# Splitting the weighing of eight experts over VectorE, ScalarE and GpSimd

## The reference, cut to what matters

```
x = inputs.reshape(-1, d)                       # the normalised residual
gate = softmax(x @ gate_w + gate_b)
weights = gate * (gate >= 0.1)                  # then divided by their sum
out = 0
for e in range(8):
    out = out + weights[:, e:e + 1] * (x @ expert_w[e] + expert_b[e])
```

## Time and profile before

| what | value |
|---|---|
| median of three runs | 2033.2 us |
| the profiled execution | 2030.23 us |
| its span | 2028.4 us |
| VectorE busy | 1732.6 us, 85% |
| ScalarE busy | 1598.6 us, 79% |
| GpSimd busy | 1500.3 us, 74% |
| the expert block | 1594.5 to 1755.8 us of the span, 161.3 us |

### The profile page before, as it was taken

One profiled execution on the slowest core, in us unless ns is written; L12 is line 12 of the kernel. 1 busy time (PEld: TensorE's weight loads), 2 busy tenths in 40 slices (PEclk: granted clock), 3 DMA queues, 4 the chain that ended last, 5 costly groups with the idle time before them and its releaser, 6 DMA issues. The chain is left out here.

```text
span 2028.4 us, 26725 instructions
## 1 busy us (share of the span) xinstructions
PE 1588.8 (78%) x8579; PEld 560.5 (28%) x8579; DVE 1732.6 (85%) x3742; ACT 1598.6 (79%) x1374; POOL 1500.3 (74%) x1026
## 2 busy tenths in 40 slices
PE   2678888887788888768888888888887587899966
PEld 1122222222222222222222222222221243366655
DVE  3789999997999999879999999999997388755556
ACT  2689999998999999979999999999999311222243
POOL 2989999997999999889999999999998001000000
PEclk7789999998999999989999999999999787877778
DMA  4100000000000000010000000000000000000001
GB/s 112 29 28 13 13 13 18 13 13 27 29 13 13 13 17 15 12 39 14 18 13 12 13 18 13 13 13 19 13 13 7 1 1 0 0 1 1 1 0 42
DMA packets 32491, 33.12 MB, mean 16 GB/s; under 512 B 5657, under 2 KB 23136, under 8 KB 32352
## 3 DMA queue, kind: packets, MB, share of 16 engines
q1 hardware_dynamic: 31056, 31.06, 5.0%
q10 hardware_dynamic: 1296, 0.35, 0.1%
HBM read 22.74 MB, written 8.39 MB: 15 GB/s over the span
## 5 line engine op out<-in xcount | busy, mean ns | idle before, releaser
L879 POOL TENSOR_TENSOR sigma_weights<-grown 128x1024 f32<-128x1024 f32 x480 | 909.7, 1899 | 0.0
L792 ACT ACTIVATE tau_weights<-ps_tau 128x1024 f32<-128x1024 f32 x512 | 720.8, 1408 | 37.4 <-PE ps_tau L424 37.3
L573 DVE TENSOR_SCALAR sigma_weights<-ps_sig 128x512 int32<-128x512 int32 x1024 | 690.6, 674 | 62.8 <-PE ps_sig L415 62.3
L778 ACT ACTIVATE sigma_weights<-sigma_weights,kernel_shape 128x2048 f32<-128x2048 f32 x256 | 611.1, 2387 | 0.2 <-POOL sigma_weights L879 0.2
L582 DVE TENSOR_TENSOR running_max<-ps_sig,running_max 128x512 f32<-128x512 f32 x896 | 604.3, 674 | 0.0
L852 POOL TENSOR_SCALAR grown<-sigma_weights,kernel_shape 128x1024 f32<-128x1024 f32 x480 | 540.1, 1125 | 78.9 <-DVE sigma_weights L573 78.4
L787 ACT ACTIVATE sigma_weights<-sigma_weights 128x2048 f32<-128x2048 f32 x256 | 588.9, 2301 | 0.0
L466 PE MATMUL ps_acc<-sigma_weights,v_heads 128*9 128x512 f32 x2048 | 533.0, 599 | 0.0
L466 PE MATMUL ps_acc<-tau_weights,v_heads 128*9 128x512 f32 x2048 | 531.5, 598 | 0.6 <-DVE sums L599 0.5
L424 PE MATMUL ps_tau<-q_operand,k_operand 128*128 128x512 bf16 x1024 | 311.2, 386 | 207.7 <-ACT tau_weights L792 200.2
L415 PE MATMUL ps_sig<-q_operand,k_operand 96*128 96x512 bf16 x1024 | 402.0, 393 | 73.1 <-DVE running_max L582 43.8
(11 more groups left out here) (169 smaller groups left out, 1440.5 us busy)
## 6 DMA issues: line engine op xcount, KB each, us to landing
q_operand<-q_parts SPq DMA_DIRECT2D x192, 48.0 KB
k_operand<-k_parts SPq DMA_DIRECT2D x64, 144.0 KB
q_parts<-parts SPq DMA_DIRECT2D x24, 128.0 KB, 2.3
k_parts<-parts SPq DMA_DIRECT2D x24, 128.0 KB, 2.3
x_res<-in_L_attn_x SPq DMA_DIRECT2D x8, 256.0 KB, 5.4
q_operand<-max_rows SPq DMA_DIRECT2D x128, 2.0 KB
out<-x_res SPq DMA_DIRECT2D x4, 512.0 KB, 3.2
experts<-in_L_ffn_expert_w SPq DMA_DIRECT2D x1, 512.0 KB
```

What stands on the lines that cost most here:

```text
L573: dve.tensor_scalar(sig[:, g % SIG_RING, cols].bitcast(I32), ps_sig[:, half, :].bitcast(I32), SIGN_OFF, None, ALU.bitwise_and).then_inc(ma ...
L778: act.activation(chunk(c), chunk(c), ACT.Ln, bias=shape[:, CHUNK * c // TB % H, 1:2]).then_inc(ln_done, 1)
L792: act.activation(tau[:, g % TAU_RING, :], ps_tau[:, :, :].rearrange("p h q -> p (h q)"), ACT.Exp, scale=float(DH) ** -0.5).then_inc(tau_do ...
L879: pool.tensor_tensor(sig[:, g % SIG_RING, :], t, t, ALU.mult).then_inc(sq_ready, 1)
```

## The change

For each pair of tiles VectorE now weighs experts 0, 1, 2, 4, 5 and 6 (`OWN = 6`). The last expert of each half (3 and 7) is read out of PSUM by ScalarE, scaled by its weight and written to a new buffer `expert_scaled` in SBUF (four operations of 128x128 for a pair). GpSimd adds the two halves to each other and then adds the sum to x (two operations of 128x256 for a pair), after VectorE's own twelve of that pair and after both bias additions. `expert_scaled` has room for one pair, so ScalarE waits for GpSimd's addition of the pair before. ScalarE reads a bank only after VectorE's last read from it, and TensorE writes a bank again only when ScalarE has also read it.

ScalarE's list is cut in pieces: the scalings stand in it at the places of the pairs, and the copies for `biases`, `project` and `gate` stand between them. GpSimd's list gets eight new operations per batch around its old two.

```diff
--- before.py
+++ after.py
@@ -946,6 +946,7 @@
         guard = sb("gate_guard", [P, TB])
         weight = sb("gate_weight", [P, TB, E])
         weight_t = sb("gate_weight_t", [E, N])
+        scaled = sb("expert_scaled", [P, 2, 2, D])
         ps_t = ctx.enter_context(nc.psum_tensor("ps_mt", [P, 2, HALF], F32))
         ps_y = ctx.enter_context(nc.psum_tensor("ps_my", [P, 2, HALF], F32))
         ps_e = ctx.enter_context(nc.psum_tensor("ps_me", [P, 2, 2, HALF], F32))
@@ -958,6 +959,9 @@
         gate_ready, gate_step, exp_ready = sem("gate_ready"), sem("gate_step"), sem("gate_exp")
         bias_ready, bias_added = sem("expert_bias_ready"), sem("expert_bias_added")
         e_ready, e_step = sem("e_ready"), sem("e_step")
+        scaled_ready, scaled_summed, scaled_added = sem("e_scaled_ready"), sem("e_scaled_summed"), sem("e_scaled_added")
+
+        OWN = 6
         GATE = 11
         block = ctx.enter_context(nc.Block())
 
@@ -981,16 +985,33 @@
                     act.activation(turned_sb[:, use, g * HALF:(g + 1) * HALF], ps_t[:, g, :], ACT.Copy)\
                        .then_inc(turned_read, 1)
 
-            def normal_and_gate(b):
+            def scale(pair):
+                def part(b):
+                    act.wait_ge(gate_step, b * GATE + GATE)
+                    wait(act, scaled_added, b * 4 + pair)
+                    for half in range(2):
+                        for t in (2 * pair, 2 * pair + 1):
+                            act.wait_ge(e_step, b * TB * OWN + (2 * OWN * pair + OWN * half + OWN - 1 + t % 2))
+                            e = 4 * half + 3
+                            act.activation(scaled[:, t % 2, half, :], ps_e[:, t % 2, half, 3 * D:4 * D], ACT.Copy,
+                                           scale=weight[:, t, e:e + 1]).then_inc(scaled_ready, 1)
+                return part
+
+            def first_norm(b):
                 take_turned(b, 0, y_ready, b * TB)
                 take_rstd(act, w, mv[:, 0], lnv[:, 0], rstd[:, 0], mv_ready[0], ln_ready[0], rstd_ready[0], b)
+
+            def second_norm(b):
                 take_rstd(act, w, mv[:, 1], lnv[:, 1], rstd[:, 1], mv_ready[1], ln_ready[1], rstd_ready[1], b)
+
+            def gate(b):
                 take_turned(b, 1, e_ready, b * 2 * TB)
                 act.wait_ge(gate_step, b * GATE + 3)
                 act.activation(prob[:, :, :], lg[:, :, :], ACT.Exp).then_inc(exp_ready, 1)
 
             act.preload_act_table_set("natural_log_exp_and_others")
-            rounds(act, [(0, take_weights), (1, normal_and_gate)])
+            rounds(act, [(0, scale(0)), (0, take_weights), (0, scale(1)), (1, first_norm), (0, scale(2)), (1, second_norm),
+                         (0, scale(3)), (1, gate)])
 
         @block.tensor
         def _(pe):
@@ -1027,7 +1048,8 @@
 
                     for half in range(2):
 
-                        wait(pe, e_step, b * TB * E + max(0, 2 * E * (pair - 1) + E * (half + 1)))
+                        wait(pe, e_step, b * TB * OWN + max(0, 2 * OWN * (pair - 1) + OWN * (half + 1)))
+                        wait(pe, scaled_ready, b * 2 * TB + max(0, 4 * (pair - 1) + 2 * (half + 1)))
                         for t in (2 * pair, 2 * pair + 1):
                             pe.matmul(ps_e[:, t % 2, half, :], turned_sb[:, 1, t * P:(t + 1) * P],
                                       w["experts"][:, 4 * half:4 * half + 4, :], start=True, stop=True).then_inc(e_ready, 1)
@@ -1054,8 +1076,7 @@
 
                 return rows[:, :].unsqueeze(1).to_broadcast([P, TB, D])
 
-            for b in range(B):
-
+            def normed(b):
                 xs = w["x"][:, bass.ds(b * TB, TB), :]
                 pool.wait_ge(yn_ready, b * TB + TB)
                 pool.wait_ge(x_ready, b)
@@ -1064,6 +1085,22 @@
                 pool.wait_ge(x_step, b + 1)
                 alone(pool, w["pool_passed"])
                 pool.tensor_tensor(xs, xs, yn[:, :, :], ALU.add).then_inc(x_ready, 1)
+
+            def add_scaled(pair):
+                def part(b):
+                    pool.wait_ge(scaled_ready, b * 2 * TB + 4 * pair + 4)
+                    alone(pool, w["pool_passed"])
+                    pool.tensor_tensor(scaled[:, :, 0, :], scaled[:, :, 0, :], scaled[:, :, 1, :], ALU.add)\
+                        .then_inc(scaled_summed, 1)
+                    pool.wait_ge(scaled_summed, b * 4 + pair + 1)
+                    pool.wait_ge(bias_added, b * 2 + 2)
+                    pool.wait_ge(e_step, b * TB * OWN + 2 * OWN * (pair + 1))
+                    alone(pool, w["pool_passed"])
+                    two = w["x"][:, b * TB + 2 * pair:b * TB + 2 * pair + 2, :]
+                    pool.tensor_tensor(two, two, scaled[:, :, 0, :], ALU.add).then_inc(scaled_added, 1)
+                return part
+
+            rounds(pool, [(0, add_scaled(0)), (0, add_scaled(1)), (1, normed), (0, add_scaled(2)), (0, add_scaled(3))])
 
         @block.vector
         def _(dve):
@@ -1130,13 +1167,13 @@
             def experts(pair):
                 def part(b):
 
-                    done = 2 * E * pair
+                    done = 2 * OWN * pair
                     if pair == 1:
                         dve.wait_ge(bias_added, b * 2 + 2)
-                    for e in range(E):
+                    for e in (0, 1, 2, 4, 5, 6):
                         for t in (2 * pair, 2 * pair + 1):
                             if e > 0:
-                                dve.wait_ge(e_step, b * TB * E + (done - 1))
+                                dve.wait_ge(e_step, b * TB * OWN + (done - 1))
                             if e % 4 == 0:
                                 dve.wait_ge(e_ready, b * 2 * TB + (4 * pair + 2 * (e // 4) + t % 2 + 1))
                             dve.scalar_tensor_tensor(out=xt(b, t), in0=ps_e[:, t % 2, e // 4, (e % 4) * D:(e % 4 + 1) * D],
@@ -1147,7 +1184,7 @@
 
             def biases(b):
 
-                dve.wait_ge(e_step, b * TB * E + 2 * E)
+                dve.wait_ge(e_step, b * TB * OWN + 2 * OWN)
                 for g in range(2):
                     dve.wait_ge(bias_ready, b * TB + 4 * (g + 1))
                     xs = w["x"][:, bass.ds(b * TB + 4 * g, 4), :]
```

## The result

The changed kernel takes 2044.84 us (median of 4 runs, 2044.43 to 2048.99), the one before 2031.58 in the same comparison. The ratio is 1.0071 with a 95% interval of 1.0051 to 1.0091: slower, by 13 us (the medians) to 14 us (the ratio). The profiled execution took 2045.11 us with a span of 2043.3, 14.9 us above the 2028.4 of before.

The account below looks back on a forecast made before the run. VectorE's list bounds the expert block, with ScalarE's copies hidden beside it. Three rounds of 43.60 us add 18.7 us and the last batch 1.9: +20.6, forecast 2051 us, own range 2045 to 2057, whole range 2038 to 2068.

Parts of the forecast that it names:

- Step 1: Round, gate to VectorE's end of the pair 0 experts: 7.89 us, against 8.87 before in batch 1.
- Step 2: Round, on to the bias addition: weights' copy, once hidden, now waits behind scalings and is paid in full, 2.25 us; before 0.43.
- Step 3: Round, bias addition to VectorE's end of the pair 1 experts: 5.83 us; before 6.70.
- Step 4: Round, on to VectorE's first y operation, its ScalarE copy now behind scalings: 2.32 us; before 0.16.
- Step 5: Round, from VectorE's y operation L1075 to the end of L1084: 7.03 us, unchanged.
- Step 6: Round, on to the statistics of the new x: 5.22 us, unchanged, GpSimd ending it; pair 2's gain becomes a longer wait.
- Step 7: Round, from the statistics of the new x to the end of L1096: 5.26 us.
- Step 8: Round, on to VectorE's end of the pair 3 experts: 3.12 us; before 4.14.
- Step 9: Round, on to the next gate: z's copy behind scalings, logits at TensorE's lower clock, 4.68 us; before -0.08.
- rival (c): TensorE's clock also falls after new idleness ahead of bias matmuls and `project`: about 5 us a batch, 2071 us; chance 0.13.
- (a): Expert block: VectorE's time alone sets it, so removed weighings gain up to 16.6 us, 2014 us; chance 0.04.
- (b): Expert block: waits grow by half the forecast because ScalarE gets its copies in earlier, +1.9 us a round, 2038; chance 0.05.

Follow-up runs that it names:

- Experiment 3: Kernel before, VectorE still weighing all eight experts, plus a tiny ScalarE operation after each pair that waits for VectorE, where the change has its scalings: 2061.22 us, ratio 1.0143.
- experiment 1: Changed kernel with ScalarE's list reordered so that all three copies (weights, attention output, z) stand ahead of the scalings: 2018.81 us, ratio 0.9943 to the kernel before.
- experiment 4: Changed kernel with only the gate's copy (turned z) ahead of the scalings of pair 3: 2033.08 us, ratio 1.0013 to the kernel before.
- experiment 5: Changed kernel with only the copy of the turned weights ahead of the scalings of pair 0: 2044.22 us, ratio 1.0056 to the kernel before.
- Experiment 2: Kernel before with experts 3 and 7 left out of VectorE's weighing and given to no other engine: 2019.35 us, ratio 0.9940.
- Experiment 8: Changed kernel with all three copies first and the last pair of the last batch weighed by VectorE alone: 2027.37 us, ratio 0.9976 to the kernel before.

## Why the prediction was right

The forecast was 2051 us, the measured time 2044.8, inside the whole range of 2038 to 2068 but just under the forecast's own, which begins at 2045. The mechanism is that of the steps; that the number came so close is partly luck, as the end of this section says. Measured in round 1 (gate at 1663.36), with the predicted value first:

| step | predicted | measured |
|---|---|---|
| 1, gate to the end of experts(0) | 7.89 | 7.25 |
| 2, to the bias addition | 2.25 | 2.18 |
| 3, to the end of experts(1) | 5.83 | 7.60 |
| 4, to y | 2.32 | 2.28 |
| 5, to the end of L1084 (now L1121) | 7.03 | 6.78 |
| 6, to the statistics of x | 5.22 | 5.22 |
| 7, to the end of z | 5.26 | 5.26 |
| 8, to the end of experts(3) | 3.12 | 3.11 |
| 9, to the gate | 4.68 | 4.62 |
| sum | 43.60 | 44.30 |

- Steps 2, 4 and 9, the three copies behind scalings, came out within 0.1 us. Experiment 3 shows that the waits cause them, experiments 1, 4 and 5 that the order does.
- Step 6, that pair 2 saves nothing because GpSimd's normalisation ends the stretch, is exact: 2.12 us of idleness for the predicted 2.1. Experiment 2 shows it without ScalarE and GpSimd's new work.
- Step 3 is the mis-sized term of the block, 1.77 us a round. I took TensorE at full clock. Here 8 matmuls took 5.40 us, and VectorE waited 1.23 us for the second tile. That is rival (c), to which I had given 0.13: it came, but only in part. The clock was low for about 3.4 us (1674.6 to 1678.0), all within experts(1), so it cost 1.8 us a batch instead of 5; the bias matmuls ran at the full clock (2.05 us), and behind the 1.65 us of idleness ahead of `project` it did not fall (2.02 us, as before). Step 1 gave 0.64 back, because the clock rose earlier while the eight expert matmuls of pair 0 ran: 5.94 us, for 6.58 in batch 0 of the kernel before, which was the pattern.
- The prices of the new operations were good: 0.364 us for 0.38 on ScalarE, 0.726 for 0.72 on GpSimd.
- The last batch lost 3.4 us and not 1.9. Its end is as predicted:

```profile
1777.11 0.63 ACT L996 ACTIVATE expert_scaled<-ps_me,gate_weight 128x128 f32<-128x128 f32 x2 [1.08 <-DVE x_res L1179]
...
1778.84 0.72 POOL L1100 TENSOR_TENSOR x_res<-x_res,expert_scaled 128x256 f32<-128x256 f32 x1 [0.20 <-POOL expert_scaled L1093]
...
1779.91 1.64 DVE L886 BATCH_NORM_STATS2 stats_c<-x_res 128x6 f32<-128x128 f32 x8 [2.58 <-PEq L925]
```

  ScalarE's last scalings, GpSimd's two additions, and VectorE idle for 2.58 us. What goes beyond the 1.9 us is mainly the low clock in experts(1) again, 1.8 us, less 0.65 won ahead of the bias addition.
- The block lost 24.1 us where I had 20.6. The program lost 14.9 in the profile because the later stages were shorter by 9.2, a term that the prediction did not have. It treated all behind the block as fixed. The total came close to the forecast by two misses against each other: with the later stages as long as in the kernel before, the same block would have given about 2054 us (2045.1 and 9.2), still inside both ranges.
- Rivals (a) and (b) are out: (a) by experiment 2, (b) by the waits. The rule of Perfetto Trace Analysis of the Trainium skill (Optimizing Scalar/DVE Operations), that moving work off a saturated VectorE may pay, is not borne out for the order of the change (24.1 us lost in the block). Once the copies stand first it is, but for little: the block is 3.5 us shorter in experiment 1.

The best version measured that computes the whole sum is experiment 1, with 0.9943 of the kernel before. Of its 13 us in the profile (span 2015.4 for 2028.4) 4.2 are won between the first gate and the end of the block; 10.2 are the shorter causal stage, which the edit did not aim at, and 1.4 are lost elsewhere. Experiment 8 has the shorter block and the longer causal stage. So the change's idea, in the right order, is worth some 4 us by these profiles (2.6 to 4.9, by experiment and by where the block is taken to begin); the rest of the gain in the median is not its own.

## What to carry to other kernels

When an idle engine is given work that waits for the busiest one, look at what stands behind it in its list: here 64 cheap operations on an engine 12% busy cost 24 us, because three copies that the busiest engine needs next were queued behind them. Put what others wait for first, and what waits for others last. Before taking work off the busiest engine, ask at each point of its list which chain will then end last; here, in round 1, three of four pairs gave next to nothing back.

## What the runs showed of the hardware

- In all four batches of the changed kernel TensorE's clock fell in the work that followed an idleness of 1.54 us (in round 1 about 3 us after that work began, at 1674.6, and it rose again at 1678.0). With the same idleness in the same place of experiment 4 it fell in three batches and not in the fourth (8 matmuls in 5.40 and in 3.70 us).
- The unchanged causal stage took either 176 or 186 us. TensorE's busy time alone differs by these 10 us (154.5 and 164.5), VectorE's and ScalarE's by nothing, and in all ten profiles the length goes with four matmuls near the stage's start (2.56 to 2.77 us, or 3.32 to 3.68). In a program of 2030 us that is 0.5%, as much as most edits here won or lost: an effect of that size has to be looked for in the stage that was edited.
